# Leaving out sixteen products on constants at the start of a one-core attention block

## What is computed

```python
x = L0_attn_x                       # 1 x 1024 x 256, float32
xn = _layernorm(x, axis=-1)
q, k, v = xn @ Wq, xn @ Wk, xn @ Wv # 16 heads of 128
q, k = rmsnorm(q, q_rms_w), rmsnorm(k, k_rms_w)
scores = einsum(q, k) * scale + alibi_bias, causal
y = rmsnorm(softmax(scores) @ v, subln_w)
x = x + y @ Wproj + fp8_rounded(xn) @ (weight * scale).T
```

## Time and profile before

| | us |
|---|---|
| median of 3 runs | 519.19 |
| lowest, highest | 518.9, 522.19 |
| the profiled execution | 518.89 |
| its span, first to last instruction | 517.1 |
| TensorE matmuls busy in it | 505.1 (98%) |
| VectorE, ScalarE, GpSimd busy | 419.6, 379.2, 349.3 |

### The profile page before, as it was taken

One profiled execution on the slowest core, in us unless ns is written; L12 is line 12 of the kernel. 1 busy time (PEld: TensorE's weight loads), 2 busy tenths in 40 slices (PEclk: granted clock), 3 DMA queues, 4 the chain that ended last, 5 costly groups with the idle time before them and its releaser, 6 DMA issues.

```text
span 517.1 us, 11927 instructions
## 1 busy us (share of the span) xinstructions
PE 505.1 (98%) x3337; PEld 466.9 (90%) x3337; DVE 419.6 (81%) x996; ACT 379.2 (73%) x894; POOL 349.3 (68%) x500
## 2 busy tenths in 40 slices
PE   7998999999999999999999999999999999999996
PEld 4987998999999899999989999999999989999885
DVE  5689789788888987888798888978878898788975
ACT  4878686787867768786776968678786876878562
POOL 6788785857858387783858758585785838758301
PEclk9999999999999999999999999999999999999999
DMA  6101001010010101001010000101001000000002
GB/s 176 53 2 42 1 1 42 3 42 0 2 41 0 41 0 41 0 0 41 0 41 0 14 27 0 41 0 41 0 0 41 0 10 0 10 3 1 1 2 82
DMA packets 18615, 10.84 MB, mean 21 GB/s; under 512 B 2208, under 2 KB 18592, under 8 KB 18592
## 3 DMA queue, kind: packets, MB, share of 16 engines
q1 hardware_dynamic: 17600, 10.49, 6.9%
q10 hardware_dynamic: 992, 0.07, 0.1%
HBM read 9.51 MB, written 1.05 MB: 20 GB/s over the span
## 4 chain that ended last, share of the span: by engine, by line
PE 88%; DVE 5%; ACT 2%; POOL 2%; issue 2%; DMA 1%; DVEq 0%; POOLq 0%
PE pT_ps L702 12%; PE qkv_ps L608 10%; PE qkv_ps L610 9%; PE qkv_ps L609 8%; PE yT_ps L610 7%; PE yT_ps L608 7%; PE yT_ps L609 7%; PE score_big L608 4%; PE score_big L610 4%; PE score_big L609 4%; PE misc L667 2%; PE score_small L609 2%; PE score_small L610 2%; PE score_small L608 2%; PE misc L608 1%
## 5 line engine op out<-in xcount | busy, mean ns | idle before, releaser
L1003 ACT ACTIVATE stage<-qkv_ps 128x384 f32<-128x384 f32 x116 | 57.1, 492 | 85.8 <-PE qkv_ps L610 85.7
L1317 DVE TENSOR_TENSOR pT_lo<-pT_ps,pT_hi 128x384 fp32r<-128x384 f32 (+2 forms) x192 | 100.2, 550 | 10.5 <-ACT pT_hi L1035 10.5
L1035 ACT ACTIVATE pT_hi<-pT_ps 128x384 fp32r<-128x384 f32 (+2 forms) x192 | 86.7, 486 | 26.1 <-PE pT_ps L702 26.0
L1025 ACT ACTIVATE probs<-probs,neg_max 128x384 f32<-128x384 f32 (+7 forms) x128 | 99.2, 776 | 5.0 <-DVE neg_max L1308 4.4
L702 PE MATMUL pT_ps<-ident,probs 128*128 128x128 f32 x576 | 85.9, 276 | 4.1 <-DVE pT_lo L1317 4.0
L608 PE MATMUL qkv_ps<-w_hi,xT_hi 128*128 128x384 f32 x240 | 87.6, 365 | 0.8 <-DVE xT_lo L1397 0.8
L610 PE MATMUL qkv_ps<-w_hi,xT_lo 128*128 128x384 f32 x240 | 81.0, 337 | 0.0
L702 PEld LDWEIGHTS pT_ps<-ident,probs 128*128 128x128 f32 x576 | 66.2, 141 | 16.2 <-ACT probs L1025 5.0
L609 PE MATMUL qkv_ps<-w_lo,xT_hi 128*128 128x384 f32 x240 | 80.6, 336 | 0.0
L608 PE MATMUL yT_ps<-pT_hi,v_hi 128*128 128x256 f32 (+1 forms) x224 | 73.1, 326 | 0.0
L610 PE MATMUL yT_ps<-pT_hi,v_lo 128*128 128x256 f32 (+1 forms) x224 | 72.0, 322 | 0.0
(11 more groups left out here) (214 smaller groups left out, 1298.4 us busy)
## 6 DMA issues: line engine op xcount, KB each, us to landing
w_raw<-in_wq SPq DMA_DIRECT2D x16, 128.0 KB, 2.2
w_raw<-in_wk SPq DMA_DIRECT2D x16, 128.0 KB, 2.3
w_raw<-in_wv SPq DMA_DIRECT2D x16, 128.0 KB, 2.3
wp_raw<-in_wproj SPq DMA_DIRECT2D x16, 128.0 KB, 2.1
acc<-in_x SPq DMA_DIRECT2D x4, 256.0 KB, 4.8
out<-acc SPq DMA_DIRECT2D x8, 128.0 KB, 2.0
w<-in_ffn_w ACTq DMA_DIRECT2D x1, 64.0 KB, 5.4
q_col<-in_q_w ACTq DMA_DIRECT2D x1, 0.5 KB, 3.0
```

What stands on the lines that cost most here:

```text
L1003: act.activation(stage_of(h, k // 2)[:, k % 2, :], qkv_bank(h, k)[:, 0:3 * D], ACT.Copy).then_inc(qkv_read, 1)
L1025: act.activation(probs[:, s % 2, 0:(i + 1) * P], probs[:, s % 2, 0:(i + 1) * P], ACT.Exp, bias=neg_max[:, par, s:s + 1], scale=-1.0, accum ...
L1035: act.activation(pT_hi[g][:, a:b, r * P:(r + 1) * P], pT_ps[(chunk0(h, s) + k) % 2][:, 0:(b - a) * P].rearrange("p (j t) -> p j t", t=P), ...
L1317: dve.tensor_tensor(pT_lo[g][:, a:b, r * P:(r + 1) * P], pT_ps[(chunk0(h, s) + k) % 2][:, 0:(b - a) * P].rearrange("p (j t) -> p j t", t=P ...
```

## The change

`WARM_UP` goes from 16 to 0: the call at line 806 then issues nothing. The two calls that issue two products each stay, as do the wait for `ident_b` and all else.

```diff
         w8T_ps = misc[:, :].bitcast(bf16)
-        WARM_UP = 16
+        WARM_UP = 0
         POOL_NORMS = (1, 3)
```

## The result

| | us |
|---|---|
| changed kernel, median of 20 runs | 522.50 (519.78 to 523.31) |
| kernel before, median of 20 runs | 520.49 (518.90 to 522.73) |
| ratio | 1.0026, 95% interval 1.0014 to 1.0038 |
| profiled execution of the changed kernel, its span | 522.45, 520.7 |

The change costs time: 2.0 us by the medians, and by the ratio 1.4 us with an interval of 0.7 to 2.0 us (0.0014 and 0.0038 times 520.5). The difference of the medians lies at the upper end of that interval. That is within 1%, as forecast. The median of before moved as well: with 20 runs it is 520.49, not the 519.19 of the first three, and its profiled execution (518.89) turns out to be its best run of the twenty.

A forecast was written before the change was run, and what follows sets the result against it. TensorE, busy 98% of the span, was taken to set the pace nearly everywhere, except mainly the start. Terms 0 + 0 + 2.33 - 0 gave +2.3 us on the profiled 518.89, so 521.2 us, range 519.4 to 523.2.

The forecast's parts named there:

- The sixteen lie off the chain; gain 0: Start, TensorE: transposes of x come earlier, but their reader on ACT is not free sooner; gain 0.
- Rival E: Start: earlier transposes help if ACT takes xT_hi ahead of its place; gain up to 1.2 us, 517.7 us, chance 0.03.
- Low clock at the transposes; cost 0: First transposes of x run at half clock; the last pair ends about 0.22 us later, which is covered; cost 0.
- the cover: Slack of 1.5 us between ACT's xT_hi pair ending at 10.85 and DVE's reader of the second starting at 12.33.
- Low clock at the projections; 2.33 us: First projections from 10.98 us: clock low for 4.66 us of dense work, matmuls 0.346 us apart, TensorE 2.33 us late.
- bounds of 1.1 to 4.3: Range in us for TensorE's lateness at the first projections, from a shorter or longer cold stretch.
- Absorbed: 0: From the first projections to the end: no later wait swallows the lateness; 0, bound 0.5 us.
- Rival B: Waits on transposed probabilities and on DVE and POOL swallow the 2.33 us by about 50 us; 519.0 us, chance 0.12.
- Clock stays low beyond 21 us (D): Transposes at 14.29 and later break the dense work, the rise starts over; slower by over 1%, chance 0.05.
- The sixteen aren't needed (C): Four products left and eight transposes raise the clock by 10.98 us anyway; 518.9 us, chance 0.08.
- a fall during the run would be expected to show, and none does: Whole run: the granted-clock column showed no fall in the profile's 40 slices, so none was counted.

The follow-up runs named there:

- e9_after: The changed kernel, nothing further altered, run again on another chip; median 522.19 us (9 runs), ratio 1.0037 to the kernel before.
- e10_small16: The changed kernel with sixteen products of 8 columns where the sixteen of 512 were; median 522.41 us (6 runs), ratio 1.0030 to the kernel before.
- e3_late12: The kernel before plus twelve constant products between the second and third projection of head 0; median 522.07 us (10 runs), ratio 1.0034.
- after: The first profile of the changed kernel, WARM_UP 0 against 16 in the kernel before; profiled execution 522.45 us, span 520.7.
- e1: The kernel before with all twenty constant products left out, the four of the two later calls too; median 521.15 us (10 runs), ratio 1.0000.
- e7_fill_only: The changed kernel plus two constant products between the first two quarters' transposes and three before the first projection; median 522.27 us, ratio 1.0029 to the kernel before.
- e11_small_fill: The kernel before plus five products of 8 columns, two between the first two quarters' transposes, three before the first projection; median 520.32 us, ratio 0.9997.
- e5_same_before: The kernel before, unedited, timed and profiled once more; median 520.60 us (10 runs), ratio 0.9994.
- e8_fill_early: The kernel before with WARM_UP 8, plus three constant products between the first two quarters' transposes and two before the first projection; median 521.28 us, ratio 1.0003.
- e2_eight: The kernel before with eight of the sixteen products kept, twelve in all; median 521.61 us (10 runs), ratio 1.0021.
- e12_fill_again: Second timing of the kernel before plus five 512-column products, two between the first quarters' transposes, three before the first projection; median 519.41 us, ratio 0.9985.

## Why the prediction was right, and where not

**The sixteen lie off the chain; gain 0.** Right. Transposes 1.15 us earlier, xT_hi not before ACT was free, first projection at 11.04 against 10.98. Rival E is out.

**Low clock at the transposes; cost 0.** Right: each group of four took 1.18 us of the timeline, the second xT_hi had to wait 0.30 us for the last of them (the forecast said 0.22), and the cover took it up.

**Low clock at the projections; 2.33 us.** The mechanism was right and the term a little small for the profiled execution: 2.64 - 0.06 = 2.58 us. Two errors in it partly offset each other: the length alone would have made 5.8 / 2 = 2.9, the pace alone 2.14. The cold stretch was longer, from 11.04 to about 16.9, 5.8 us instead of 4.66; and the low pace was 0.320 us, not my 0.346. Of the two values weighed, that of the Trainium skill ("TensorE: Matmul & The Clock Gate", section "Wait — 56ns, not 53.3ns?"), columns over clock, was the better one: 5.8 x (1 - 0.173 / 0.320) = 2.7. Doubling the pace at the high clock failed since that pace, 0.173, is itself above 384 columns at 2.4 GHz (0.160). In e9_after the term was 1.3 us, in e10_small16 1.9: inside the bounds of 1.1 to 4.3.

**Absorbed: 0.** Right, and shown with the clock up in e3_late12. Rival B is out.

**Clock stays low beyond 21 us (D).** Did not happen in any of the five profiles without the sixteen dense products (after, e1, e7, e9, e10). **The sixteen aren't needed (C).** Out: every profile with four or fewer dense products in front was cold at 11 us.

**What I missed.** The sum was made against one execution in which the sixteen did their work in full, and the step "a fall during the run would be expected to show, and none does" took one run for all. In 41% of the runs of before the mean clock tells of a fall, and in the one that was profiled it came at 11.5 us, right behind the stretch from the first transposes to the first projection (8.59 to 10.98 in the earlier trace rows), in which TensorE has little to do. So before is on average about 0.41 x 1.6 = 0.7 us worse for that cause than a run that keeps its clock, and the change takes away that much less. On the median it is less, 0.4 us: 520.55 for all 85 runs against 520.14 for the unmarked 50. But these 50 are still 1.2 us above the profiled 518.89, and that larger part is open; the tail and a somewhat later first projection (11.08 in e11_small_fill, 11.30 in e3_late12) are seen in profiles and were not counted. Unmarked runs alone put the change at 522.40 - 520.14 = 2.3 us. The predicted 521.2 lay 1.3 below the measured median and its difference to before (2.0 against the first median of 519.19) met the 2.0 of the medians, partly by luck: both ends had moved up by the same 1.3. The ratio puts the difference at 1.4.

## To carry to other kernels

Constant products that raise TensorE's clock cost nothing here as long as the engine would otherwise wait, but they pay only if the clock holds until the real matmuls: look at what TensorE does between the last of them and the first long run of work, and try dense products in those gaps too (five more gave 1.0 us here, part of it for a reason not found). One profile is one draw: compare each run's mean granted clock with its time before a mechanism is priced from one trace.

## What the runs showed of the hardware

- Where dense work began at 1.97 us and went on for 5 us or more, the granted clock rose between 4.7 and 7.6 us on the timeline (e5_same_before, e8_fill_early). Without that it rose 1.7 us (e7_fill_only) to 5.8 us (after) after the first projection began. It differs between runs of the same kernel.
- It fell to 1.2 GHz behind stretches in which TensorE was busy for 1.19 of 2.40 us (e5_same_before) and 1.43 of 2.90 us (e2_eight), and near the end behind one of 2.31 of 2.90 us (e7_fill_only). It came back 3.4 us after the fall in one profile (e5_same_before, 11.5 to 14.9), 6.8 in another (e2_eight, 10.5 to 17.3).
- The granted-clock column shows 1.00 ahead of the first rise although matmuls of 512 columns started 0.43 us apart; the spacing has to be read there.
- Sixteen matmuls of 8 columns, with four of 512 behind them, did not raise the clock by the first projection (e10_small16); five in the gaps did not keep it up in 5 of 11 runs, by their mean clock (e11_small_fill).
- A 16 KB load of code among the last stores went with 0.5 (e12_fill_again) to 1.7 us (e9_after) more of tail than in the six profiles without it.
